# The last phase of a fused four-layer transformer: ScalarE and VectorE trade two PSUM copies

## The reference

```
x = x + xattn0(ln(x), ctx);   x = x + moe0(ln(x))            # 8 experts, top 2
x = x + xattn1(ln(x), ctx);   x = x + quantised_ffn(ln(x))   # scale is a max over everything
x = x + xattn2(ln(x), ctx);   x = x + slot_ffn(ln(x))        # 16 heads of 8 columns
x = x + xattn3(ln(x), ctx);   x = x + shared + moe3(ln(x))   # 16 heads of 64 columns
```

```
q = x @ Wq;  k, v = split(context @ Wkv)          # 16 heads, 64 columns each: 1024 columns
attn = softmax(q k^T * 64**-0.5);   out = (attn v) @ Wout + bout
```

## Time and profile before

| what | value |
|---|---|
| timed runs | 2093.86, 2100.3, 2102.59 us; median 2100.3 |
| the profiled execution's own time | 2098.33 us |
| its span (first to last instruction) | 2096.5 us |
| granted TensorE clock, mean over the span | 0.97 of 2.4 GHz |
| busy share of the span | PE 88%, DVE 71%, ACT 62%, POOL 30% |
| chain that ended last, by engine | PE 38%, DVE 9%, ACT 5%, issue 4%, POOL 1% |
| k copy on VectorE | 64 times, median 682 ns |
| v copy on ScalarE | 64 times, median 597 ns |

### The profile page before, as it was taken

How to read it: one execution, slowest core, us unless ns; L and a number is a source line. 1 busy time by engine, 2 the same in 40 slices (tenths; PEclk the granted TensorE clock), 3 DMA queues, 4 the chain that set the end, 5 groups by cost and what they waited for, 6 DMA issues and landing times.

```text
span 2096.5 us, 50110 instructions
## 1 busy us (share of the span) xinstructions
PE 1850.7 (88%) x17731; PEld 1506.8 (72%) x17731; DVE 1484.3 (71%) x3865; ACT 1304.1 (62%) x4466; POOL 621.6 (30%) x618
## 2 busy tenths in 40 slices
PE   2998999989999987777789889999999998888879
PEld 2877888778878775656666667777778776777665
DVE  5898887878878886757766675767757565655456
ACT  1987766656757786556677756666666654544432
POOL 0003031222412220033434343353443423333321
PEclk9999999999999999978899999999999999999999
DMA  8013355454644100400000021223212223232351
GB/s 247 17 32 106 118 162 151 117 158 137 175 142 142 30 27 24 143 15 20 30 7 15 6 66 46 81 67 98 93 54 70 82 79 91 83 98 74 104 158 41
DMA packets 128790, 178.45 MB, mean 85 GB/s; under 512 B 10144, under 2 KB 89824, under 8 KB 128288
## 3 DMA queue, kind: packets, MB, share of 16 engines
q1 hardware_dynamic: 120864, 159.51, 25.2%
q0 software_dynamic: 7680, 15.74, 2.4%
HBM read 141.26 MB, written 33.95 MB: 84 GB/s over the span
## 4 chain that ended last, share of the span: by engine, by line
PE 38%; DVE 9%; ACT 5%; issue 4%; POOL 1%; DVEq 0%; ACTq 0%
PE ps L1672 5%; PE ps L1969 5%; PE ps L1917 3%; PE ps L1722 3%; PE ps L1910 3%; PE ps L1706 3%; ACT pb L2118 2%; PE ps L1891 2%; PE ps L1713 2%; PE ps L1683 2%; PE ps L1732 2%; DVE nm L2497 1%; PE ps L1740 1%; PE ps L1939 1%; PE ps L1883 1%
## 5 line engine op out<-in xcount | busy, mean ns | idle before, releaser
L2118 ACT ACTIVATE pb<-ps,nm 128x128 f32<-128x128 f32 x1024 | 364.1, 378 | 194.3 <-DVE nm L2497 194.3
L2166 POOL TENSOR_TENSOR pb<-pb,rcs 128x512 f32<-128x512 f32 x256 | 268.8, 1051 | 657.9 <-DVE rcs L2505 657.2
L986 ACT ACTIVATE pb<-pb,nm 128x128 f32<-128x128 f32 x1024 | 312.9, 393 | 32.2 <-DVE nm L1221 30.4
L2522 DVE COPY pt<-ps 128x512 f32<-128x512 f32 x128 | 88.3, 690 | 197.9 <-PE ps L1969 197.8
L2118 ACT ACTIVATION_READ_ACCUMULATOR pb<-ps,nm 128x1 f32 x1024 | 222.3, 217 | 0.0
L2497 DVE TENSOR_REDUCE nm<-ps 128x8 f32<-128x1024 f32 x128 | 155.9, 1218 | 60.7 <-PE ps L1917 38.6
L1969 PE MATMUL ps<-w,pb 128*128 128x128 f32 x1024 | 167.1, 288 | 23.2 <-ACT pt L2126 10.8
L1221 DVE TENSOR_REDUCE nm<-pb 128x8 f32<-128x1024 f32 x128 | 156.2, 1220 | 4.4
L1969 PEld LDWEIGHTS ps<-w,pb 128*128 128x128 f32 x1024 | 121.2, 147 | 47.1 <-ACT pt L2126 20.3
L870 PE MATMUL ps<-w,pb 128*128 128x128 f32 x1024 | 141.2, 279 | 7.7 <-ACT pb L986 7.3
L2126 ACT ACTIVATE pt<-ps 128x512 f32<-128x512 f32 x128 | 77.0, 602 | 92.9 <-PE ps L1969 92.7
(11 more groups left out here) (381 smaller groups left out, 4403.0 us busy)
## 6 DMA issues: line engine op xcount, KB each, us to landing
big<-in_we SPq DMA_DIRECT2D x92, 514.0 KB
big<-in_we SPq DMA_DIRECT2D x109, 384.0 KB
sorted_out<-big SPq DMA_DIRECT2D x27, 256.0 KB
big<-sorted_in SPq DMA_DIRECT2D x7, 960.0 KB, 6.3
sorted_in<-big SPq DMA_DIRECT2D x4, 1472.0 KB, 12.2
big<-sorted_in SPq DMA_DIRECT2D x20, 256.0 KB, 3.6
hidden<-h_all SPq DMA_DIRECT2D x7, 512.0 KB, 2.9
h_all<-hidden SPq DMA_DIRECT2D x7, 512.0 KB, 3.8
```

What stands on the lines that cost most here:

```text
L986: m = a.activation(pb[:, n % 2, k * S:(k + 1) * S], pb[:, n % 2, k * S:(k + 1) * S], ACT.Exp, bias=nm[:, n % 2, k:k + 1])
L2118: m = a.activation(pb[:, n % 2, e * S:(e + 1) * S], ps[:, score_bank(n) + half, k * S:(k + 1) * S], ACT.Exp, bias=nm[:, n % 2, e:e + 1], a ...
L2166: g_.tensor_tensor(p4, p4, r4.unsqueeze(2).to_broadcast([P, 4, S]), ALU.mult).then_inc(n2["p_normed"], 1)
L2522: v.tensor_copy(pt[:, p % 2, 4 * S:8 * S], ps[:, BANK_T, :]).then_inc(n2["p_lo"], 1)
```

## The change

The two engines trade the copies. The copy of k, at place 2 of an even step, goes from VectorE to ScalarE. The copy of v, at place 2 of an odd step, goes from ScalarE to VectorE. Semaphores, waits and buffers stay the same, and TensorE's order is untouched.

```diff
 # ScalarE, work(place, hs), after the copy of q
-                    chunk = V_AT.get(hs)
                     if chunk and place == 2:
                         g, c = chunk
-                        a.wait_ge(n2["v_psum"], IC3 * g + c + 1)
+                        a.wait_ge(n2["k3_psum"], IC3 * g + c + 1)
                         before = number[(3, g, c - 2)] if c >= 2 else number[(3, g - 1, c + IC3 - 2)] if g else None
                         if before is not None:
-                            a.wait_ge(n2["pv"], before + 1)
-                        a.activation(v3[c % 2], ps[:, BANK_A, :], ACT.Copy).then_inc(n2["v_row"], 1)
+                            a.wait_ge(n2["scores"], before + 1)
+                        a.activation(k3[c % 2], ps[:, BANK_A, :], ACT.Copy).then_inc(n2["k3_col"], 1)
 # VectorE, work(place, hs), after the products of the expert tiles
-                    chunk = QK_AT.get(hs)
+                    chunk = V_AT.get(hs)
                     if chunk and place == 2:
                         g, c = chunk
-                        v.wait_ge(n2["k3_psum"], IC3 * g + c + 1)
+                        v.wait_ge(n2["v_psum"], IC3 * g + c + 1)
                         before = number[(3, g, c - 2)] if c >= 2 else number[(3, g - 1, c + IC3 - 2)] if g else None
                         if before is not None:
-                            v.wait_ge(n2["scores"], before + 1)
-                        v.tensor_copy(k3[c % 2], ps[:, BANK_A, :]).then_inc(n2["k3_col"], 1)
+                            v.wait_ge(n2["pv"], before + 1)
+                        v.tensor_copy(v3[c % 2], ps[:, BANK_A, :]).then_inc(n2["v_row"], 1)
```

## The result

The changed kernel took 2110.0 us as the median of ten runs (2099.8 to 2116.6), the kernel before 2098.9 us in its ten. The ratio of the runs is 1.0039, with a 95% interval of 1.002 to 1.0058: 8.2 us more, between 4.2 and 12.2 (the two medians lie further apart, 11.1 us). The change costs about what was predicted. That is inside the 0.5% taken as no change, though the interval does not reach 1.

A forecast was written before the change was run, and what follows sets the result against it. TensorE sets the pace, so time changes only where it waits; +7 (A) + 4 (B) - 4 (C) = +7 us on 2098.3 us gives 2105 us, with own range 2099 to 2112 and overall range 2091 to 2116.

The forecast's parts named there:

- A: Stretch 1045 to 1250 us, scores made a step ahead, 14 chunks: 7 us longer.
- C: Stretch 1655 to 2000 us, only every second step filled, 24 chunks: 4 us shorter.
- The price of a ready copy: Where both engines stand ready, v costs TensorE 0.18 us more per chunk and k 0.18 us less.
- The two extra terms: In A, first k copy about 0.5 us later behind ScalarE's work; k behind table load and first Gelu, +1.4 us.
- The pairs: In A, 14 step pairs with later maxima: six at 0.75 us, seven others together 0.7; 5.2 us longer.
- B: Stretch 1250 to 1655 us, expert tiles between units, 26 chunks: six odd steps 0.7 us longer each, +4 us.
- the v side: In C, eight steps where ScalarE reached v late gain 0.95 us each: 7.6 us.
- the k side: In C, four k copies come off VectorE's chain, 0.5 us each: 2.0 us gained.
- The bound: In C, of q's 18.9 us waiting 13 must stay as copy and release; q side gives at most 6.
- TensorE's largest wait goes: Faster rival: VectorE takes each v when complete, C gives 9 us, time 2089; chance 0.13.
- The maxima hold everything: Slower rival: v copy delays maxima in A (15 us) and B (4 us), C gains nothing, 2117; chance 0.20.
- Nothing moves: Rival: copies are needed only two to four steps later, swap costs what it gives, 2098 to 2100; chance 0.13.

The follow-up runs named there:

- v moved by choice: Against the kernel before, from chunk 40 on, v on VectorE only at places 1, 2, 5, 7 of each group of eight; k unchanged: 2091.6 us.
- before's 35: 35 runs of the unchanged kernel before, on the one chip that also timed four experiment kernels: median 2101.9 us.
- swap late: The full trade of k and v only for chunks 40 to 63, otherwise the kernel before: 2100.2 us, ratio 0.9993.
- chosen: Against the kernel before, from chunk 40 on, all k on ScalarE, v on VectorE only at places 1, 2, 5, 7 of eight: 2092.4 us, ratio 0.9962.
- after's second: The changed kernel, unchanged, run once more for a second trace: 2112.6 us.

## Why the prediction was right

**What bounds and where.** TensorE's waits set the time, and three stretches behave in three ways: held by the table of differences, with +6.5, +3.9 and -3.4 us where +7, +4 and -4 were forecast. That is measured, though low clock had to be taken out step by step to see it. That the three add up to just the +7 of the forecast is luck: A came out 0.5 lower and C 0.6 higher than the sum had them, and larger errors inside A and C cancel.

**The price of a ready copy** was the term that was mis-sized. 0.18 us was read from start to start of two different copies. Measured, a ready v costs 0.10 more on VectorE (the first two steps with only v moved, +0.10 each) and a ready k 0.10 less on ScalarE (5.53 to 5.43 above). From the start of VectorE's v copy to q it is 0.74 us, not the 0.83 of its k copy. The Trainium skill's estimate (VectorE: DVE Perf Modes, section on the TRN2 errata) gave 0.09, and the 0.10 of these runs agrees with it. As the term was small it moved the sum little, but the q waits in A came out at 0.75 us each (8.2/11) where 0.8 or more was said.

**A.** The rows shown with the prediction do not give its 0.9 us for the maxima: a v copy from 1119.6 to 1120.3 makes them 0.6 later. The other 0.3 is a piece of quantising (L2248) that stands between the two on VectorE. Measured from the v copy's start, the maxima are 0.89 later, so the number held. The two extra terms were exact: k of chunk 0 +0.49 (0.5 said), k behind the Gelu +1.45 (1.4 said). The pairs gave 6.5 - 0.58 - 1.55 = 4.4 where 5.2 was said. Of the first eleven steps four more lie between 0.79 and 1.13, and one later with 0.92 (six pairs between 0.5 and 1.0 were said). Three steps were shorter by 0.34, 0.86 and, less before's low clock, 0.4 us, which lies outside the -0.2 allowed. The 0.86 comes with k's leaving VectorE, to which the prediction gave no worth in A: the same step is 0.8 shorter, less its low clock, with only k moved, and unchanged with only v moved. The 0.34 comes with either half alone (0.36 and 0.40), and its cause stays open. That both halves are needed for the loss was in the working (maxima late, then k behind the copy), and the runs with one half show it.

**B.** Six steps, 0.7 each: they were six, at 0.70 and 0.85, 4.6 us together. The steps behind them gave back 0.4, and k's leaving VectorE gave 0.12 in three steps, where nothing was said for k. The other odd steps cost nothing.

**C.** Ten steps were 0.86 to 1.23 us shorter, 9.8 us in all; 7.6 + 2.0 was said for eight steps and four k copies. With only v moved the same ten steps give the same 9.8, so the v side was too small by 2.2, and the k side too large by 1.1: -0.9 alone, where -2.0 stood, and at two other steps than those of the earlier trace rows. The losses are eight steps with 5.9 us (the step with before's two low stretches put at 0.75, from 3.2 less the 2.44 seen) and 0.5 in small ones; 5.8 was said, but with only v moved they are 7.0 with the small ones, where the whole change has 6.4. These errors cancel. The bound was wrong too: it kept 20 x 0.65 = 13 us of waiting as copy and release, so that the q side could give back no more than 6. With v moved by choice q waits 8.8 us in all, the same with k moved and without, and v alone then gives 7.1: where v is copied early its release can be hidden behind an expert product, as in the rows at 1816.56, and q then waits for nothing.

**The rivals.** *TensorE's largest wait goes* is wrong for the trade as made, since A and B lose; but in C its mechanism is real, and where v is moved only in the right steps it gives -8 us. *The maxima hold everything* needed 15 us in A; 6.5 came. Its upper bound of 0.9 + 0.18 a pair was reached in no more than two of the first eleven steps. *Nothing moves* would describe the timing of the two halves, not that of the whole.

**The timed runs.** Those of after spread over 16.8 us and before's ten over 10.7, but before's 35 spread over 17.5, so the spread is not the change's. In each kernel the time falls as the granted clock of the run rises: 2116.6 us at 0.963 and 2099.8 at 0.973 for after. A straight line with one slope for all timed kernels (1.5 us for each 0.001 of clock) puts them, at equal clock, +5.7 us (after), -1.1 (only k), +4.0 (only v), -3.3 (swap late) and -8.2 (chosen) against before's 35, each within 1.3 us or so. The steps without low clock say +7.0, -1.5, +4.3, -3.4 and -8.35. After's ten were not timed together with these 35 of before, so its figure is the weakest of the five.

**What stays open** is whether the change brings low clock of its own. The mean granted clock of after's ten runs, 0.9666, is near the 0.9673 of before's 35. But in the 2.32 us wait of L1732 low clock set in, 0.2 to 0.3 us before the wait ended, in two of four traces that have that wait (17.1 us in after's second, 10.2 us with only k moved), and at that place in none of the eight without it. That is suggestive of a second cost of the change, but too few traces to call it shown.

## What to carry to other kernels

A copy that two engines can take is not priced by its duration but by what stands in front of it and behind it on each engine at each step: the same trade cost 0.85 us in one step and gave 1.2 in another, so decide it per step and not per kernel. Two moves that are harmless alone can make one chain together: check the late engine of the first against the queue that the second enters. When single executions differ by more than the change, compare distances between the same instruction's starts, step by step, and set aside the steps whose granted clock differs.

## What the runs showed of the hardware

Low clock is short and costs by the step. In the second trace of after (columns as in the table of stretches) and in the first of before:

```profile
1070.30:1087.20 16.90, 16.11 (x104) 12.26 (x104) 7.55 (x27) 8.06 (x35) 3.21 (x3) 0.51 0.00 1
```

```profile
1701.60:1704.80 3.20, 3.20 (x16) 3.16 (x16) 2.50 (x10) 0.60 (x1) 0.00 (x0) 0.50 0.00 0
```

The means of the earlier trace rows, 0.99 and 1.00, hid them: I had written that the clock gives nothing and takes nothing, and in C of before it took 4.4 us. TensorE at 1.2 GHz shows as busy in each of these rows (3.20 of 3.20 us), so busy time does not give them away either; the granted clock of a narrow window does. One such stretch cost 1.2 to 1.6 us. In before each of the four sets in during or at most 2.0 us after idle time of TensorE of 0.97 to 1.93 us; but the longest idle time in this phase, 2.0 us that end at 1252.0 us, is followed by none.

Everything else repeats closely. Over 63 steps the two traces of before agree to 0.02 us each. Where one kernel leaves a stretch untouched and no low clock differs, A, B or C come out within 0.08 us of before.
